# Norms on ScalarE, a series by one scan, and the B/C convolution behind a single projection

## The reference

```
h   = relu(tanh(conv9(x) * scale) + bias)              # 248 rows of 128 a sequence
z, xBC, dt = split(layernorm(h) @ in_proj)             # 256, 384 and 4 columns
xBC = silu(depthwise_conv4(xBC) + conv_b)              # xs 256, B 64, C 64 columns
dt  = softplus(dt + dt_bias);  decay = exp(dt * A)
S_t = decay_t * S_{t-1} + (dt_t * x_t) B_t;  y_t = S_t C_t
y   = rmsnorm((y + D * x) * silu(z)) * norm_w
h   = h + y @ out_proj
g   = layer_norm(layernorm(h));  gates = softmax(g @ router / 0.7), top 2 of 16
h   = h + x' + moe(g) + ffn(layer_norm(moe(g)))        # x' = layernorm(h)
```

## Time and profile before

| | us |
|---|---|
| median of the runs | 1109.75 (1108.16 to 1110.27) |
| the profiled execution | 1112.74 |
| its span in the trace | 1111.0 |
| PE busy | 948.3 |
| DVE busy | 746.7 |
| POOL busy | 572.2 |
| ACT busy | 441.8 |

### The profile page before, as it was taken

One profiled execution on the slowest core, in us unless ns is written; L12 is line 12 of the kernel. 1 busy time (PEld: TensorE's weight loads), 2 busy tenths in 40 slices (PEclk: granted clock), 3 DMA queues, 4 the chain that ended last, 5 costly groups with the idle time before them and its releaser, 6 DMA issues. The chain is left out here.

```text
span 1111.0 us, 22688 instructions
## 1 busy us (share of the span) xinstructions
PE 948.3 (85%) x6371; PEld 795.0 (72%) x6372; DVE 746.7 (67%) x2288; ACT 441.8 (40%) x1068; POOL 572.2 (51%) x531
## 2 busy tenths in 40 slices
PE   0499999999999999999887429999999999388887
PEld 0377877877777777778665229999999999266665
DVE  4348779788797797978866615555555555488884
ACT  3233443343433333423322215555555555144443
POOL 3044444665676556775655735555555555243342
PEclk9899999999999999999986659999999999699999
DMA  6400000000000000000036422222222221223331
GB/s 134 104 20 10 1 10 11 29 20 22 17 29 29 22 24 12 29 20 17 12 95 201 137 69 61 55 63 60 63 66 62 66 62 49 74 56 91 92 92 37
DMA packets 71868, 58.97 MB, mean 53 GB/s; under 512 B 18992, under 2 KB 61291, under 8 KB 71808
## 3 DMA queue, kind: packets, MB, share of 16 engines
q1 hardware_dynamic: 63264, 41.88, 14.4%
q0 software_dynamic: 8544, 16.34, 4.4%
HBM read 35.62 MB, written 23.81 MB: 53 GB/s over the span
## 5 line engine op out<-in xcount | busy, mean ns | idle before, releaser
L1429 POOL DMA_INDIRECT y_tokens<-arena x139 | 155.9, 1122 | 144.7 <-DVE arena L1452 111.3
L1416 ACT ACTIVATE arena<-psum,arena 128x128 f32<-128x128 f32 x556 | 158.6, 368 | 132.0 <-PE psum L1390 130.8
L1390 PE MATMUL psum<-arena 128*128 128x128 f32 x1112 | 155.9, 284 | 3.5 <-DVE arena L1447 1.2
L1390 PEld LDWEIGHTS psum<-arena 128*128 128x128 f32 x1112 | 137.1, 194 | 16.2 <-issue 8.3
L1403 PE MATMUL psum<-arena 128*128 x1112 | 147.8, 275 | 0.4 <-ACT arena L1416 0.4
L1043 POOL DMA_INDIRECT x_slots<-arena,idx x128 | 127.3, 994 | 35.9 <-issue 35.9
L1444 DVE COPY arena<-arena 128x644 f32 x139 | 69.3, 499 | 109.5 <-DVE arena L1452 89.8
L1403 PEld LDWEIGHTS psum<-arena 128*128 128x128 f32 x1112 | 136.0, 193 | 0.6 <-issue 0.6
L623 PE MATMUL psum<-hnT_hi,w_tap_hi 128*128 128x496 f32 x192 | 80.3, 418 | 0.0
L1152 DVE TENSOR_TENSOR_SCAN arena<-psum,arena 124x496 f32<-124x496 f32 x64 | 72.4, 1173 | 6.7 <-PE psum L736 6.7
L624 PE MATMUL psum<-hnT_lo,w_tap_hi 128*128 128x496 f32 x192 | 75.8, 395 | 0.0
(11 more groups left out here) (249 smaller groups left out, 2051.2 us busy)
## 6 DMA issues: line engine op xcount, KB each, us to landing
arena<-x_slots SPq DMA_DIRECT2D x139, 64.5 KB
arena<-y_tokens SPq DMA_DIRECT2D x16, 448.0 KB
arena<-in_x SPq DMA_DIRECT2D x16, 256.0 KB, 2.9
out_tokens<-arena SPq DMA_DIRECT2D x16, 224.0 KB
arena<-in_ew SPq DMA_DIRECT2D x1, 2304.0 KB
y_tokens<-arena POOLq DMA_INDIRECT x139
x_slots<-zero_src SPq DMA_DIRECT2D x33, 64.5 KB, 2.7
arena<-in_x SPq DMA_DIRECT2D x4, 512.0 KB, 6.7
```

What stands on the lines that cost most here:

```text
L1390: last = nc.tensor.matmul(psum[:, 2 + b.q % 2, k * 128:(k + 1) * 128], w1_blk[b.q % 4][:, k * 128:(k + 1) * 128], hT[b.q % 2], start=True, ...
L1416: last = nc.scalar.activation(EHT[t.q % 2][:, k * 128:(k + 1) * 128], psum[:, 2 + t.q % 2, k * 128:(k + 1) * 128], ACT.Silu, bias=w1_blk[t ...
L1429: nc.gpsimd.indirect_dma_start(out=y_tokens, out_offset=bass.IndirectOffsetOnAxis(ap=xb[t.q][:, F:F + 1].bitcast(i32), axis=0), in_=YO[t.q ...
```

## The change

The B and C chunk is projected once, without taps (`bc_projection`, 3 matmuls in place of 12), at the place where z0 stood. ACT (`bc_begin`) writes the last tap and the bias to a new tile `bc_sum`; DVE (`bc_taps`) adds the three others, shifted by one to three tokens, from PSUM; ACT (`bc_silu`) makes B and C. The other chunks go in the order x0, x1, z0, z1. `w_tap` shrinks from 384 to 256 columns a tap. `norm` and `normed` leave DVE for ACT, four activations each with a column for scale and one for bias; the bias, minus mean times the power, is made on POOL, as are `r1p` and `nmr`, which DVE made before. `dt_rest` puts the terms of the series through one `tensor_tensor_scan` over 16 x 8 elements with coefficients that are set once.

```diff
+    NK = 8
...
+                                 (cw_bc[:, :], conv_w[256 * KC:384 * KC].rearrange("(p k) -> p k", k=KC)),
...
-                    last = nc.vector.tensor_tensor(w_tap[:, k, :], w_in[:, DI:DI + 384], cwv[:, k, :],
+                    last = nc.vector.tensor_tensor(w_tap[:, k, :], w_in[:, DI:DI + 256], cwv[:, k, 0:256],
...
-        chunks = (("z", 0, 3), ("x", 0, 2), ("x", 1, 2), ("z", 1, 3), ("bc", 2, 3))
+        chunks = (("x", 0, 2), ("x", 1, 2), ("z", 0, 3), ("z", 1, 3))
...
+                def bc_projection(b):
+                    later(pe, S.ip_used, 4 * b)
+                    product(psum[:, 3, 0:UT], [v[:, 512:640] for v in w_in2],
+                            [v[:, :, PADL:] for v in hnT2[b % 2]], True, True).then_inc(S.bc_psum, 1)
+
                 def projection(b, k, d):
                     what, part, bank = chunks[k]
                     if k == 0:
-                        later(pe, S.ip_used, 5 * b)
-                    if k == 1:
-                        later(pe, S.ip_used, 5 * b - 2)
+                        later(pe, S.ip_used, 4 * b - 2)
                         if d is not None:
                             later(pe, S.up_used, 2 * d - 1)
+                    if k == 1:
+                        pe.wait_ge(S.ip_used, 4 * b + 1)
                     if k == 2:
-                        pe.wait_ge(S.ip_used, 5 * b + 2)
+                        pe.wait_ge(S.bc_used, b + 1)
                     if k == 3:
-                        pe.wait_ge(S.ip_used, 5 * b + 1)
-                    if k == 4:
-                        pe.wait_ge(S.ip_used, 5 * b + 4)
+                        pe.wait_ge(S.ip_used, 4 * b + 3)
                         if d is not None:
                             pe.wait_ge(S.up_used, 2 * d + 2)
                     o = psum[:, bank, 0:UT]
...
-                    pe.wait_ge(S.ip_used, 5 * b + 3)
+                    pe.wait_ge(S.ip_used, 4 * b + 2)
...
-                    if b is not None: dt_projection(b, t); projection(b, 0, None)
+                    if b is not None: dt_projection(b, t); bc_projection(b)
                     if a is not None: x_transposes(a)
-                    if b is not None: projection(b, 1, d)
+                    if b is not None: projection(b, 0, d)
                     if a is not None: conv(a, b)
                     if d is not None: hh_transposes(d, a, t)
                     if c is not None: mix(c, 0)
                     if c is not None: scores(c, 1); decays(c, 1)
                     if m is not None: ranks(m, d)
                     if d is not None: logits(d)
-                    if b is not None: projection(b, 2, None); projection(b, 3, None); x_rows(b)
+                    if b is not None: projection(b, 1, None); projection(b, 2, None); x_rows(b)
                     if d is not None: shared_up(d, b)
                     if d == UNITS - 1: ranks(len(GROUPS) - 1, d)
                     if c is not None: mix(c, 1)
-                    if b is not None: projection(b, 4, d)
+                    if b is not None: projection(b, 3, d)
...
+                def norm(a):
+                    act.wait_ge(S.rstd_ready, a + 1)
+                    later(act, S.hnT_psum, a)
+                    for j in range(4):
+                        last = nc.scalar.activation(hn[:, j, :], Hb[:, 4 * F * a + j * F:4 * F * a + (j + 1) * F],
+                                                    ACT.Identity, scale=rstd[:, j:j + 1], bias=nmn[:, j:j + 1])
+                    last.then_inc(S.hn_ready, 1)
+
+                def normed(d):
+                    act.wait_ge(S.rs8_ready, d + 1)
+                    if d >= NXS:
+                        act.wait_ge(scattered[d % NXS], 128 * (d // NXS))
+                    for j in range(4):
+                        last = nc.scalar.activation(x_st[d % NXS][0:CH, j, 0, 0:F],
+                                                    Hb[:, 4 * F * d + j * F:4 * F * d + (j + 1) * F],
+                                                    ACT.Identity, scale=rs8[:, 4 + j:5 + j], bias=nm2[:, j:j + 1])
+                    last.then_inc(S.xst_ready, 1)
+
...
+                def bc_begin(b):
+                    act.wait_ge(S.bc_psum, b + 1)
+                    later(act, S.bct_ready, b)
+                    nc.scalar.activation(bc_sum.rearrange("p b t -> p (b t)"), psum[:, 3, 0:UT], ACT.Identity,
+                                         scale=cw_bc[:, KC - 1:KC], bias=cb[:, 2:3]).then_inc(S.bc_begun, 1)
+
+                def bc_silu(b):
+                    act.wait_ge(S.bc_used, b + 1)
+                    i = bc_sum.rearrange("p b t -> p (b t)")
+                    nc.scalar.activation(BT[b % 2], i[0:64, :], ACT.Silu)
+                    nc.scalar.activation(CT[b % 2], i[64:128, :], ACT.Silu).then_inc(S.bct_ready, 1)
 
...
                     a, b, c, d = at(t, 0), at(t, 1), at(t, 2), at(t, 3)
+                    if b is not None: bc_begin(b)
+                    if a is not None: x_copy(a)
+                    if d is not None: normed(d)
                     if b is not None: silu(b, 0)
-                    if a is not None: x_copy(a)
-                    if b is not None: silu(b, 1)
                     if d is not None: stage(d)
+                    if b is not None: bc_silu(b)
                     if a is not None: convT_copy(a)
                     if d is not None: hhT_copy(d)
                     if a is not None: tanh(a); relu(a)
                     if c is not None: square(c, 0)
-                    if b is not None: silu(b, 2); silu(b, 3)
+                    if b is not None: silu(b, 1); silu(b, 2)
                     if d is not None: shared_silu(d)
+                    if a is not None: norm(a)
                     if c is not None: square(c, 1)
-                    if b is not None: silu(b, 4)
+                    if b is not None: silu(b, 3)
                     if d is not None: residual_input(d)
                     if a is not None: hnT_copy(a)
...
                 def rstd_of(a):
                     pool.wait_ge(S.stats_ready, a + 1)
+                    later(pool, S.hn_ready, a)
+                    nc.gpsimd.tensor_scalar(neg[:, :], mv[:, :, 0], -1.0, 0.0, ALU.mult, ALU.add)
                     link(pool, S.pool_link, nc.gpsimd.tensor_tensor(ve, mv[:, :, 1], eps_row[0:CH, 0:4], ALU.add))
-                    nc.gpsimd.tensor_tensor(rstd, ve, minus_half[0:CH, 0:4], ALU.pow)\
-                        .then_inc(S.rstd_ready, 1)
+                    link(pool, S.pool_link, nc.gpsimd.tensor_tensor(rstd, ve, minus_half[0:CH, 0:4], ALU.pow))
+                    nc.gpsimd.tensor_tensor(nmn[:, :], neg[:, :], rstd, ALU.mult).then_inc(S.rstd_ready, 1)
...
+                        pool.wait_ge(S.ip_used, 4 * c + 4)
...
                 def rs8_of(c):
                     pool.wait_ge(S.ve8_ready, c + 1)
-                    nc.gpsimd.tensor_tensor(rs8[:, :], ve8[:, :], minus_half[0:CH, 0:8], ALU.pow)\
+                    later(pool, S.xst_ready, c)
+                    g = slice(4 * c, 4 * c + 4)
+                    nc.gpsimd.tensor_scalar(neg8[:, :], MV[:, g, 0], -1.0, 0.0, ALU.mult, ALU.add)
+                    link(pool, S.pool_link, nc.gpsimd.tensor_tensor(rs8[:, :], ve8[:, :], minus_half[0:CH, 0:8],
+                                                                    ALU.pow))
+                    nc.gpsimd.tensor_tensor(nm2[:, :], neg8[:, :], rs8[:, 4:8], ALU.mult)
+                    nc.gpsimd.tensor_tensor(nmr[:, g], neg8[:, :], rs8[:, 0:4], ALU.mult)
+                    nc.gpsimd.tensor_scalar(r1p[:, g], rs8[:, 0:4], 1.0, 1.0, ALU.mult, ALU.add)\
                         .then_inc(S.rs8_ready, 1)
...
-                    own(V.tensor_tensor(ss, ee, rq, ALU.mult))
-                    own(V.tensor_tensor(s2, ss, ss, ALU.mult))
-                    own(V.tensor_scalar(pa, s2, 1.0 / 15, None, ALU.mult))
-                    src, dst = pa, pb
-                    for k in (13, 11, 9, 7, 5, 3):
-                        own(V.scalar_tensor_tensor(dst, src, 1.0 / k, s2, ALU.add, ALU.mult))
-                        src, dst = dst, src
-                    own(V.scalar_tensor_tensor(tt, src, 1.0, ss, ALU.add, ALU.mult))
-                    own(V.tensor_scalar(qq, uu, 0.0, None, ALU.max))
-
-                    V.scalar_tensor_tensor(dt[b % 2], tt, 2.0, qq, ALU.mult, ALU.add)\
+                    own(V.scalar_tensor_tensor(ss, ee, 2.0, rq, ALU.mult, ALU.mult))
+                    over_k = ss.unsqueeze(2).broadcast_to([CH, 16, NK - 1])
+                    own(V.tensor_tensor(factor[:, :, 1:NK], over_k, over_k, ALU.mult))
+                    own(V.tensor_tensor_scan(series.rearrange("p n k -> p (n k)"),
+                                             factor.rearrange("p n k -> p (n k)"),
+                                             coef.rearrange("p n k -> p (n k)"), 0.0, ALU.mult, ALU.add))
+                    own(V.tensor_tensor(tt, series[:, :, NK - 1], ss, ALU.mult))
+
```

(18 more changed lines are left out.)

68 lines of the change are left out of this document (25 added, 43 removed).

## The result

The changed kernel is slower: 1123.75 us (median of 4 runs, 1119.64 to 1124.17) against 1110.01 (4 runs of before in the same group); ratio 1.0116, interval 1.009 to 1.0141 (the two medians divided give 1.0124). The forecast was 1115.5 in 1104 to 1124: right in its sign, and less than half of the size, 5.8 us for 13.7. That it lies in the range is in part luck: it is 0.25 us under the upper end, half way from the forecast to the rival *Worse* (1132), whose reasons aren't what happened. The profiled execution is the fastest of the four, 1119.64 us, so its trace shows only +6.9 us against the 1112.74 of before; the other three had a granted clock of 0.939 where this one had 0.942, and took 4 us more.

A forecast was written before the change was run, and what follows sets the result against it. POOL's queue, 17.4 us from rs8_of to the first gate, was taken to set steps 6 to 15. Terms without the clock summed to -0.4 us, extra clock falls +6.2: +5.8 on 1109.75 gives 1115.5 us, range 1104 to 1124.

The forecast's parts named there:

- Worse: Rival: small POOL operations 1.8 us in all, waits of 3.5 us with a fall in nearly each; 1132; chance 0.12.
- steps 0 and 1: First two loop turns: hn_transposes waits for norm, 0.5 us later by POOL and 0.5 by ACT; +2.0 us.
- step 2: Loop turn 2: -0.43 us from output and +0.2 from conv_rows, put at 0.
- steps 3 and 4: Loop turns 3 and 4: -0.43 us from output, +0.2 from conv_rows, put at -0.25 each.
- step 5: Loop turn 5, DVE bound with routing: -0.6 - 0.75 and some chance PE's slow stretch goes; -1.6 us.
- steps 6 to 15: Ten loop turns: POOL's additions +0.9 each, less 0.43 (even) or 0.75 (odd): +3.0 us; six clock falls for two: +6.2.
- step 16: Loop turn 16: normed done about 2 us earlier on ACT, then POOL's queue binds: -1.0, output -0.4; -1.4 us.
- step 17: Last loop turn: the 7.14 us wait of hh_transposes shrinks until DVE's decayed scores bind; -2.0 us.
- experts and FFN: MoE and final FFN, from 655 us on: not touched by the change, so no difference.
- PE bound: Rival: PE is the bound after all, so all 33 us come back; 1077; chance 0.03.
- Faster by the tail: Rival: gain between x_rows and the residual exceeds POOL's additions, if below 0.6 us; -4.7 us, 1105; chance 0.15.
- No difference: Rival: POOL's 0.9 us is right but the clock falls no more often; -0.4 us, 1109.4; chance 0.20.

The follow-up runs named there:

- 1.: Kernel before with only the four small POOL operations in rs8_of added and DVE's two for r1p and nmr removed: ratio 1.0126 to the kernel before.
- 2.: Kernel before with POOL's eight scatters of a step spread over its queue in four pairs: ratio 0.9922 to the kernel before.
- 4.: The changed kernel unaltered, run again for a second trace: ratio 1.0126 to the kernel before.
- 8.: Kernel before with both norms on ACT and their small operations on POOL, B and C still three products: ratio 1.0157 to the kernel before.
- 10.: Kernel before with norms on ACT, scatters spread, and 9 useless products in the first-unit step: ratio 0.9806 to the kernel before.
- 11.: Kernel before with norms on ACT, scatters spread, and POOL serving rstd_of ahead of decay_of in the first-unit step: ratio 0.98 to the kernel before.
- 9.: Kernel before with both norms on ACT, their small operations on POOL, and the scatters spread in four places: ratio 0.9865 to the kernel before.
- experiment 7: The changed kernel with both norms back on DVE, keeping the single BC projection, taps and series by one scan: ratio 1.0224 to the kernel before.

## Why the prediction was right, and where its size was not

By its own terms, profiled execution against profiled execution, in us:

| term | forecast | measured | from |
|---|---|---|---|
| setup | -0.8 | -0.85 | first x transposes |
| steps 0 and 1 | +2.0 | +2.06 | 75.13 - 73.92, less the setup |
| step 2 | 0 | +4.29 | first `rs8_of` 106.18 to 111.68, less the 1.21 |
| steps 3 and 4 | -0.5 | -1.04 | 31.94, 31.62 to 31.43, 31.09 |
| step 5 | -1.6 | -1.99 | 35.80 to 33.81 |
| steps 6 to 15 | +3.0 and clock +6.2 | +3.71 | 341.18 to 344.89 |
| step 16 | -1.4 | -0.03 | 33.65 to 33.62 |
| step 17 | -2.0 | -2.47 | 33.84 to 31.37 |
| scatters at the end | +0.9 | +0.79 | last one 648.84 to 653.31 |
| experts and FFN | 0 | +2.40 | the span's +6.87, less the 4.47 |

**What held.** The bound and the mechanism: POOL's queue from step 6 on, shown by 1. (its operations alone) and, for the even steps, by 2. (the queue cleared, and step 4's length comes back). What binds the odd ones beside it, VectorE's work and what it waits for, isn't taken apart. The rival "PE bound" (1077) fell with the 33.9 us of steps with 2 us less of PE work. "Faster by the tail" needed POOL's additions below 0.6 us; they were 1.04. "No difference" needed a clock that falls no oftener; 4. and 8. have four and seven falls in ten steps, against two.

**What was mis-sized: the clock, which I had put in steps 6 to 15 alone.** In step 1 the forecast has the wait (0.84 and 1.0 us later `norm`), but counts only its length. The 2.05 us that B and C give up lie right ahead of the transposes of hn and join it: 3.84. Behind it the clock falls; 10. and 11. show that this costs 4.6 us, and in the profiled pair it is 4.7 from the transposes of hn to the next `x_rows` (23.28 for 18.55), of which +4.29 are left at the first `rs8_of`. And by 9. the later norm alone is enough to make it fall, with the nine products in place. The argument was on the page of the forecast itself (falls behind 2.1 us, none behind 1.6), but I applied it to one wait only.

**In steps 6 to 15** two errors met. Without falls the ten steps came to about +1.1 us instead of +3.0: even steps +0.25 to +0.4, odd ones -0.1 to 0 (POOL's chain +1.04, but 0.43 and more given back at `output` and behind). The falls came to +2.6 in this trace (5.8 us in three steps against 3.2 in two) instead of +6.2; in the trace of 4. the four steps with one are 36.70, 35.48, 36.72 and 35.50, 8.9 us above 33.88. So the forecast's +6.2 is near the trace of 4. (+5.7), but by fewer and longer falls, three and four at 1.4 to 2.9 us each where it had six at 1.54, and in odd steps too, where it had none; the profiled execution was a lucky one. The profiled times differ by 6.9 us and the medians by 13.7, since the traced execution is 4.1 us under its median and that of before 2.7 over its own.

**Step 16.** PE's wait before `hh_transposes` went from 2.79 to 0.54, as forecast, but the next one, at `x_rows`, grew to 4.08, and the transposes behind it ran at the lower level (1.97): what one wait gave, the next took.

**Open.** The 2.4 us in the experts and the FFN, whose code isn't changed. The forecast had this term at nothing, for that reason alone. From the start of PE's first expert matmul to that of its last it is 289.3 us before, 291.8 after, 291.5 in 4. and 290.3 in 9. It isn't one wait: it builds up over the stage, eight blocks taking 16.4 us before and 16.6 to 16.7 after. The series by one scan wasn't measured apart: seven operations end 1.9 us after the first, as against 3.05, and in experiment 7, which has it, VectorE is the bound all the same.

## What to carry to other kernels

Before moving work, find the queue that sets the period and count what the change puts into it: four operations of 0.2 us on GpSimd, ahead of a queue without a gap, cost 0.6 to 0.95 us a step (1.), and 2 us off TensorE gave half a microsecond in the steps that it bounds. Then list every wait of TensorE that grows, in the ramp-up too, and price each with the slow stretch that may follow it, not with its length; where one grows from under 1 us to about 2, as in step 1 here, look for an engine that can serve its releaser first (11.). This was worth 6 us for a reordering of four small operations. And with equal steps take more than one trace, since the number of falls differed between the two executions traced here.

## What the runs showed of the hardware that I had not expected

- Useless matmuls can pay: 9 of 0.23 us in each step (21 in one) made the changed kernel with spread scatters faster, from 0.9972 to 0.9876, and 9 in one single step took 0.6% off (9. to 10.).
- The clock's fall costs more than the wait ahead of it: in the first-unit step 4.6 us behind 1.79 us (9. against 10. and 11., from the transposes of hn to the next `x_rows`).
- A 124x4 operation on GpSimd takes 0.20 us and the next starts 0.15 to 0.17 later, little more than VectorE's 0.16 to 0.17 for most of its own.
- The chips differ in one place: on those of the first and third group (before at 1128.63 and 1125.61 us) VectorE stands still for 10 to 18 us in each of the eight kernels traced, once, before it adds the last unit's shared result (L1255 in 11., 16.0 us, at 621 us), with no engine of the core that the trace gives as releaser; none of the six traces of the other two groups has it. Times of different chips are not to be compared here, ratios on one chip are.
